# Two convolutions and a per-token MLP: group sums taken earlier, transposes spread out, four normalised chunks on ScalarE

## The reference

```python
x = x + conv3x3(_gn(x), L0)        # + bias
x = x + conv3x3(_gn(x), L1)
h = gelu(einsum("bend,edf->benf", _gn(x), w1) + b1)   # 8 experts (the channel), D=256, F=1024
x = x + einsum("benf,efd->bend", h, w2) + b2
x = x + conv3x3(_gn(x), L3)
```

## Time and profile before

| | us |
|---|---|
| median of 3 runs | 558.48 |
| lowest and highest | 556.39, 563.66 |
| the profiled execution | 555.82 |
| its span in the profile | 554.0 |

### The profile page before, as it was taken

The page is one execution under the profiler, slowest core; times in us unless marked ns, Lnnn a source line. Parts: engine busy times, 40 slices in busy tenths (PEclk is TensorE's granted clock), DMA queues, the critical chain, the costliest instruction groups (busy, mean ns, idle before and its releaser), DMA issues.

```text
span 554.0 us, 9155 instructions
## 1 busy us (share of the span) xinstructions
PE 514.7 (93%) x3374; PEld 258.8 (47%) x3374; DVE 371.8 (67%) x637; ACT 295.3 (53%) x363; POOL 170.2 (31%) x188
## 2 busy tenths in 40 slices
PE   0778999996979999999999999999999998999995
...
DMA packets 13880, 57.41 MB, mean 104 GB/s; under 512 B 3084, under 2 KB 3212, under 8 KB 10764
## 3 DMA queue, kind: packets, MB, share of 16 engines
...
HBM read 30.03 MB, written 8.39 MB: 69 GB/s over the span
## 4 chain that ended last, share of the span: by engine, by line
PE 64%; DVE 18%; ACT 6%; POOL 4%; DMA 3%; issue 3%; SPq 1%; ACTq 1%; DVEq 0%; POOLq 0%
PE PS L1119 27%; PE PS L1093 26%; DVE X L749 6%; DVE ST L710 6%; PE PS L995 3%; PE PS L988 2%; POOL XN L397 2%; PE PS L1050 2%; ACT SCR L509 2%; DMA X<-x 2%; ACT XN L504 2%; PE PS L1066 2%; PE PS L1149 1%; DVE X L767 1%; DVE SM L725 1%
## 5 line engine op out<-in xcount | busy, mean ns | idle before, releaser
L1093 PE MATMUL PS<-XT,W1S 128*128 (+1 forms) x768 | 171.9, 383 | 2.8 <-POOL XT L446 2.5
L1119 PE MATMUL PS<-HID,W2S 128*128 128x512 f16 x720 | 159.5, 379 | 1.6 <-DVE W2S L774 1.6
L550 ACT ACTIVATE SCR<-PS,CONST 128x512 f32<-128x512 f32 x128 | 87.0, 685 | 64.8 <-PE PS L1093 28.2
L1093 PEld LDWEIGHTS PS<-XT,W1S 128*128 128x128 f16 x768 | 75.6, 99 | 92.1 <-issue 5.8
L1119 PEld LDWEIGHTS PS<-HID,W2S 128*128 128x128 f16 x720 | 70.4, 98 | 82.9 <-issue 1.8
L397 POOL TENSOR_TENSOR XN<-SCR,XN 128x1024 f16<-128x1024 f32 (+1 forms) x61 | 100.4, 1669 | 16.0 <-ACT SCR L509 15.8
L774 DVE SCALAR_TENSOR_TENSOR W2S<-W2F,W2S 128x2048 f16<-128x2048 f32 x10 | 22.9, 2291 | 114.6 <-ACT W2S L546 114.6
L374 POOL MEMSET XN<- 128x128 f16 x6 | 2.8, 458 | 304.3 <-PE PS L1119 304.0
L710 DVE BATCH_NORM_STATS2 ST<-X 128x6 f32<-128x512 f32 x128 | 81.6, 681 | 9.2 <-DMA X<-x 8.0
L504 ACT ACTIVATE XN<-X,SC 128x1024 f16<-128x1024 f32 (+1 forms) x61 | 64.1, 1050 | 23.2 <-POOL SC L388 18.7
L749 DVE SCALAR_TENSOR_TENSOR X<-PS,X 128x512 f32<-128x512 f32 x96 | 59.7, 680 | 19.1 <-PE PS L1010 19.0
...
## 6 DMA issues: line engine op xcount, KB each, us to landing
...
```

Source lines behind the costliest of these rows:

```text
L550: act.activation(SCR[:, ft % 2, 0:CH], bank(ft % G_RING), ACT.Gelu, bias=BT[:, ds(e * FT + ft, 1)], scale=1.0 / (XS * WS)).then_inc(gelu_o ...
L1093: mm = pe.matmul(bank(ft % G_RING), W1S[:, w, h * NF + ft * P:h * NF + (ft + 1) * P], rhs, start=(n == 0), stop=(n == 3 * DH - 1))
L1119: mm = pe.matmul(bank(G2_BANK + h), W2S[:, w, ft * NW + h * P:ft * NW + (h + 1) * P], HID[slot][:, part, ft], start=(ft == 0 and part == 0 ...
```

## The change

1. **Step 0's thirds.** The four DMAs of the first half's thirds leave ScalarE's queue (`THIRDS_BY_ACT`) and are issued by SyncE behind its four of the columns.
2. **Group sums.** From step 5 on (`EARLY_SUMS`) `group_mean` stands behind the first `tiles` of the step instead of behind the second four centres, and `group_variance` behind the seventh centre instead of behind the second `tiles`. VectorE's `deviation` comes right behind the first four updates, `variance` after two chunks of statistics. Three chunks of statistics of step 7 move into the first hidden product, and with them `aggregate(11)`.
3. **Single places.** T(0) to T(15) no longer stand in pairs and fours, except T(0), T(1) and T(14), T(15); some are between two centres, some in the midst of `tiles`. VectorE's `xt_low` follow. VectorE's part of W1 is now ahead of the updates (7, 4..7) and behind `xt_low(12)`; ScalarE's is two chunks later (behind chunk 11).
4. **Who does what.** Chunks 8 to 11 are normalised by ScalarE (`PRE_BY_ACT`). The low parts of 18, 20 and 22 go from VectorE to GpSimd. The whole copies now use the second half of each `SCR` slot, so the first gelu no longer waits for all of GpSimd's low parts.
5. **Third output product.** Its eight result transposes stand at parts 1, 3, 7, 9, 11, 13, 14, 15 instead of at each odd one.

```diff
-THIRDS_BY_ACT = ((0, 0), (10, 0), (10, 1), (11, 0), (11, 1))
+THIRDS_BY_ACT = ((10, 0), (10, 1), (11, 0), (11, 1))
...
-PREPARED = {(6, 0, 1): (0, 1), (6, QUAD, 0): (2, 3), (6, QUAD, 1): (4, 5),
-            (7, 0, 0): (6, 7), (7, 0, 1): (8, 9), (7, QUAD, 0): (10, 11),
-            (7, QUAD, 1): (12, 13, 14, 15)}
-POOL_LOW = (3, 5, 7, 9, 11, 13, 15)
+MIDST, BEHIND = QUAD, QUAD + 1
+PREPARED = {(6, 0, BEHIND): (0, 1),
+            (6, QUAD, 1): (2,), (6, QUAD, 3): (3,), (6, QUAD, MIDST): (4,), (6, QUAD, BEHIND): (5,),
+            (7, 0, 0): (6,), (7, 0, 2): (7,), (7, 0, 3): (8,), (7, 0, MIDST): (9,),
+            (7, 0, BEHIND): (10,),
+            (7, QUAD, 1): (11,), (7, QUAD, 3): (12,), (7, QUAD, MIDST): (13,),
+            (7, QUAD, BEHIND): (14, 15)}
+EARLY_SUMS = 5
+PRE_BY_ACT = (8, 9, 10, 11)
+POOL_LOW = (3, 5, 7, 9, 11, 13, 15, 18, 20, 22)
...
     @block.gpsimd
-        low_parts(7, 0, 3)
+        low_parts(7, 0, 2)
         scale_and_bias(8)
         for j in range(2):
             pre_chunk(j)
-        low_parts(7, 3)
+        low_parts(7, 2)
...
         for j in range(2, NCH):
             pre_chunk(j)
+        scale_and_bias(9)
         xt_low(3)
+        pre_chunk(12)
+        pre_chunk(13)
         xt_low(5)
-        scale_and_bias(9)
...
+        for m in (7, 9, 11):
+            xt_low(m)
+        scale_and_bias(10)
+        for j in range(2):
+            pre_chunk(2 * NCH + j)
+        for m in (13, 15):
+            xt_low(m)
         for j in range(2, NCH):
-            pre_chunk(NCH + j)
-            if j in (4, 6):
-                xt_low(5 + j)
-        xt_low(13)
-        xt_low(15)
-        for b in range(2, NB):
-            scale_and_bias(8 + b)
-            for j in range(NCH):
-                pre_chunk(NCH * b + j)
+            pre_chunk(2 * NCH + j)
+            if j in (3, 5, 7):
+                xt_low(2 * NCH + j - 1)
+        scale_and_bias(11)
+        for j in range(NCH):
+            pre_chunk(3 * NCH + j)
...
     @block.scalar
         for m in range(2 * NCH):
             xt_high(m)
-            if m == NCH + 1:
+            if m in (4, 5, 6, 7):
+                pre_chunk(m + 4)
+            if m == NCH + 3:
                 split_high(W1F, W1S, w1_in, w1_hi, 0)
...
     @block.vector
+        def sums_and_stats(n, g):
+            deviation(n)
+            for m in prepared(g, 0, (BEHIND,)):
+                xt_low(m)
+            stats(g, 0, 2)
+            variance(n)
...
+        updates(5, 0)
+        sums_and_stats(8, 5)
+        stats(5, 2, 2)
+        updates(5, QUAD)
+        stats(5, QUAD, QUAD)
+        aggregate(9)
+        updates(6, 0)
+        sums_and_stats(9, 6)
+        xt_low(2)
+        stats(6, 2, 2)
+        xt_low(4)
+        updates(6, QUAD)
+        xt_low(6)
+        stats(6, QUAD, QUAD)
+        aggregate(10)
+        xt_low(8)
+        updates(7, 0)
+        sums_and_stats(10, 7)
+        xt_low(12)
+        split_low(W1F, W1S, w1_in, w1_hi, w1_ok, 0)
+        updates(7, QUAD)
+        xt_low(14)
+        stats(7, 2, 3)
...
         def in_first(ft):
             xt_low(2 * NCH + ft)
+            if ft < 3:
+                conv_stats(7, 5 + ft)
+            if ft == 2:
+                aggregate(11)
             if ft == 3:
                 deviation(11)
+            if ft == 4:
+                variance(11)
             if ft == 5:
-                variance(11)
                 w2_parts(0)
...
     @block.tensor
                 for k in range(QUAD):
                     centre(g, i + k)
+                    if i > 0 and k == 2 and g >= EARLY_SUMS:
+                        group_variance(3 + g)
+                    prepare(g, i, k)
-                tiles(g, i)
-                if i > 0:
+                tiles(g, i, lambda: prepare(g, i, MIDST))
+                if i > 0 and g < EARLY_SUMS:
                     group_variance(3 + g)
+                if i == 0 and g >= EARLY_SUMS:
+                    group_mean(3 + g)
+                prepare(g, i, BEHIND)
...
         def in_third_output(ft):
-            m = 2 + (h * FT + ft) // 2
-            if ft % 2:
+            places = (1, 3, 7, 9, 11, 13, 14, 15)
+            if h * FT + ft in places:
+                m = 2 + places.index(h * FT + ft)
                 result_transposes(m // NCH, m % NCH)
```

69 lines of the change are left out of this document (38 added, 31 removed).

## The result

The changed kernel takes 559.83 us (median of 20 runs, 556.26 to 564.05), the kernel before 558.49 (20 runs, 555.02 to 563.66). The ratio is 1.0038 with a 95% interval of 1.002 to 1.0056: 2.1 us slower, where the prediction had 1.9 us faster. Within 2% it is the same kernel; the small difference is clear of the noise, and its sign is the other one. The ratios leave out executions that took over 1.5% more than the fastest of the same kernel: one each of `x2_places` (907.87 us), `x4_sums6` (1380.14), `x7_fill_h` (563.76), `x8_warm5` (561.02) and `ts_after` (560.34), and two of `x11_all` (562.78, 1903.89). The profiled execution took 559.81 us (span 558.0), 4.0 more than the one before (555.82, 554.0).

What follows compares the result with a forecast made beforehand. TensorE was busy 93% of the span, so only its idle and slow time could be won. The terms -2.8 + 1.5 - 0.6 = -1.9 us, from a base of 557.4, gave 555.5 us; range 549.5 to 560.5.

Steps and rivals of the forecast that it cites:

- rival (a): Ahead of T(24) in the first output product: the clock falls, costing +2.5 us, 558.0 us in all; chance 0.2.
- Part 1, -2.8: Step 0: without ScalarE's DMA issues GpSimd runs on without a gap and borders land earlier, -2.8 us.
- The lower bound, 0: Step 0's thirds: no gain if the late first half costs what the rest gives; the other bound was 3.1 us.
- Part 2, +1.3: Step 5: L725 waits 1.5 us for GpSimd's running instruction, so the last centre and step 6 start 1.3 us later.
- the early scale isn't used up: Steps 5 and 6: GpSimd does image 0's scale a half-step earlier, but TensorE's first transposes come only at 108 us.
- Part 3, hidden product 1.8 us earlier: Steps 5 to 7: the hidden product starts at 136.7 instead of 138.53 us, despite VectorE's waits for transposes.
- Part 4: Hidden product to T(24): 1.7 us given back and T(24) 1.5 us later, at 162.3 instead of 160.82 us.
- Part 5, -0.6: Third output product: TensorE's 1.57 us wait for VectorE shrinks, and the chain behind gains some 0.6 us.

Runs made afterwards that it cites:

- x2_places: The kernel before with only the third output product's result transposes at their new places; ratio 0.9988.
- x4_sums6: The changed kernel with step 5's group sums at their old place, steps 6 and 7 keeping the new ones; ratio 1.0106.
- x7_fill_h: The changed kernel with 14 extra, overwritten matmuls ahead of the first hidden product; ratio 1.0032.
- x8_warm5: The kernel before with SyncE issuing all step 0 thirds and 5 instead of 7 unread warm matmuls ahead of step 0's third centre; ratio 0.9948.
- ts_after: The changed kernel with the deviation's last instruction rewritten to one SBUF input and two scalars by pointer; ratio 0.9989.
- x11_all: The changed kernel with 5 warm matmuls, the low part of 22 moved back, 14 extra matmuls ahead of the hidden product and 6 in the last step; ratio 0.9992.
- the rewritten instruction: The kernel before with the deviation's last instruction taking one input and two scalars by pointer instead of two SBUF inputs; ratio 0.9988.

## Why the prediction was wrong

Forecast -1.9 us, measured +2.1. The range (549.5 to 560.5) holds 559.83 only because it is wide; of the 4.3 us between 555.5 and 559.83, 1.1 is the base (557.4, and 558.49 in 20 executions). What happened is rival (a) and more. Two steps failed: part 3's gain ahead of the hidden product, which isn't there, and the clock at T(24), which the sum put at nothing.

**Part 1, -2.8.** Its mechanism was right and the trace after shows it (2.75 at U5). As a mean over executions it came out smaller: 2.3 us alone, which the interval (0.9 to 3.6) doesn't tell from 2.8, and 1.0 within the change, the difference of two ratios whose intervals overlap. What it had wrong is "GpSimd goes on without a gap", taken as pure gain: three of six traces lost it again. I had read L725's 0.22 us against 1.11 as a wait for GpSimd and used it in step 5, but not in step 0, where the same instruction had met an idle GpSimd only because of the gap that part 1 closes. The lower bound, 0, was given for another reason and is what the profiled execution of part 1 alone shows.

**Part 2, +1.3.** Right: 1.32 us of wait, from U5 to step 6 1.47 us longer, and by the rewritten instruction it is GpSimd's hold. Wrong in the side remark that the early scale isn't used up.

**Part 3, hidden product 1.8 us earlier.** This step failed: it is 0.07 earlier, and the four other traces of the changed kernel's parts 2 and 3 with the old instruction and step 5's early sums agree (43.39 to 43.45 us from U5 to H; a fifth, `x11_all`, has 43.41; 43.48 before). VectorE was to reach the low part of 12 at 130.4; in the same frame it did at 131.8 (129.05 + 2.75), and the rest of the way took 0.4 us longer than forecast. I had waits for T(4) and T(6) but no sizes: VectorE's order now has low parts ahead of updates and statistics (waits of 1.63 and 0.61 us), and the half-step with the first of them is 1.65 us longer than before. That those waits are the cause is read from the trace; no run put the low parts back alone.

**Part 4.** The 1.33 us for `MV`, and the held-off low part of 22 with a gap of 2.24 us at T(24), are as forecast (1.3; "2 to 3"). T(24) was to be 1.5 us late and is 2.87, since part 3's gain wasn't there to be given back. Rival (a), with 0.2, came true in three of five traces; its condition, a gap past 2.06 us, was met, its price was 1.7 us, not 2.5. The sum had taken the clock there as unchanged.

**Part 5, -0.6.** 0.9 in the traces, 0.7 by the ratio.

In sum, against the kernel before: part 1 -1.0, parts 2 to 4 up to T(24) +2.9, the clock +1.7 in three of five (1.0), part 5 -0.9 make +2.0, beside the measured 2.1. That the two nearly meet is in part luck: part 1's 1.0 and the share of three in five are known to a microsecond at best. The 3 us more at the end of the profiled execution are no part of it: 1.4 of wait for border rows and 1.7 of clock, and kernels without any of parts 2 to 4 show the same (part 1 alone: 2.29 us, then 14.7; the rewritten instruction alone: 2.61, 14.6), others with them don't (`ts_after`: 1.49, 13.0). That it comes equally often in both kernels was not measured.
